# An attention kernel that also makes the residual sum, its statistics and its router products

## The reference, cut to what matters

```python
x = x + 0.5 * ffn(layernorm(x))         # x: (8, 2048, 256)
x = x + attention(layernorm(x))         # 8 heads of 32, rank 32 projections
x = x + 0.5 * ffn(layernorm(x))

def ffn(x):                             # x is already normalized
    scores = x @ w_router
    _, idx = top_k(scores, 128)         # 128 of 2048 tokens of each batch
    x_sel = take(x, idx)
    ...                                 # small attention and gated FFN on x_sel
    return x.at[idx].set(x_sel + x_attn + x_ff)
```

## Time and profile before

| what | us |
|---|---|
| median of 3 runs | 4373.87 |
| the profiled execution, its own time | 4375.15 |
| its span, first to last instruction | 4373.6 |
| s2 with its entry (3847.0 to 4018.6) | 171.6 |
| t2 (4018.6 to 4096.0) | 77.4 |
| f2 (4096.0 to the end) | 278 |
| a steady unit of `attend` | 46.7 |

### The profile page before, as it was taken

One profiled execution on the slowest core, in us unless ns is written; L12 is line 12 of the kernel. 1 busy time (PEld: TensorE's weight loads), 2 busy tenths in 40 slices (PEclk: granted clock), 3 DMA queues, 4 the chain that ended last, 5 costly groups with the idle time before them and its releaser, 6 DMA issues. The chain is left out here.

```text
span 4373.6 us, 59760 instructions
## 1 busy us (share of the span) xinstructions
PE 3589.1 (82%) x20178; PEld 1423.8 (33%) x20178; DVE 3267.7 (75%) x4504; ACT 3208.9 (73%) x6587; POOL 2938.5 (67%) x1094
## 2 busy tenths in 40 slices
PE   0167685599999999999999999999999999900376
PEld 0133463233333333333333333333333333300243
DVE  9644575788888888888888888888888888368544
ACT  5044474498898998998998898998988988723143
POOL 0011000399999999999999999999999999952211
PEclk9998898699999999999999999999999999955588
DMA  8200699689999999999999999999999998877100
GB/s 280 89 3 5 212 395 341 130 180 192 208 199 205 206 199 205 198 209 203 200 208 195 207 198 205 206 199 207 197 208 204 201 205 186 169 249 249 39 5 5
DMA packets 335171, 809.45 MB, mean 185 GB/s; under 512 B 27084, under 2 KB 210912, under 8 KB 271136
## 3 DMA queue, kind: packets, MB, share of 16 engines
q0 software_dynamic: 66432, 475.04, 53.9%
q1 hardware_dynamic: 222496, 284.46, 22.2%
q10 hardware_dynamic: 45952, 46.27, 3.0%
HBM read 198.90 MB, written 136.48 MB: 77 GB/s over the span
## 5 line engine op out<-in xcount | busy, mean ns | idle before, releaser
L1682 ACT ACTIVATE at_probs<-at_ps_s 128x512 f32<-128x512 f32 x4096 | 2262.1, 615 | 254.7 <-PE at_ps_s L1792 247.3
L1541 POOL TENSOR_TENSOR at_pool_sum<-at_pool_sum,at_probs 128x2048 f32<-128x2048 f32 x448 | 2173.0, 4850 | 30.9 <-DMA at_probs<-at_probs 23.5
L1571 DVE TENSOR_REDUCE at_part_max<-at_ps_max 128x3 f32<-128x1536 f32 x1024 | 1801.3, 1759 | 426.8 <-PE at_ps_max L1715 426.7
L1792 PE MATMUL at_ps_s<-at_qs,at_ks 97*128 97x512 f32 (+1 forms) x4096 | 1523.4, 451 | 6.2 <-ACT at_probs L1682 4.9
L1761 PE MATMUL at_ps_acc<-at_probs,at_v 128*32 128x512 f32 x8192 | 1091.8, 605 | 0.9 <-ACT at_probs L1682 0.9
L1792 PEld LDWEIGHTS at_ps_s<-at_qs,at_ks 97*128 97x128 f32 (+1 forms) x4096 | 626.1, 188 | 1102.4 <-ACT at_probs L1682 815.9
L1573 DVE TENSOR_REDUCE at_part_max<-at_max_copy 128x1 f32<-128x512 f32 x1024 | 692.1, 676 | 0.0
L1634 ACT COPY at_max_copy<-at_ps_max 128x512 f32<-128x512 f32 x1024 | 610.1, 596 | 102.2 <-PE at_ps_max L1715 102.1
L1715 PE MATMUL at_ps_max<-at_ks,at_qs 32*128 32x512 f32 x4096 | 525.4, 500 | 83.0 <-DMA at_ks<-qk_parts 49.3
L1520 POOL DMA_DIRECT2D at_probs<-at_probs x448 | 399.3, 891 | 284.5 <-ACT at_probs L1682 236.7
L1715 PEld LDWEIGHTS at_ps_max<-at_ks,at_qs 32*128 32x128 f32 x4096 | 197.8, 183 | 442.1 <-issue 386.0
(11 more groups left out here) (193 smaller groups left out, 2550.0 us busy)
## 6 DMA issues: line engine op xcount, KB each, us to landing
at_probs<-at_probs POOLq DMA_DIRECT2D x448, 1024.0 KB, 8.3
qk_parts<-pr_hi SPq DMA_DIRECT2D x32, 1024.0 KB, 12.0
qk_parts<-pr_lo SPq DMA_DIRECT2D x32, 1024.0 KB, 12.5
at_qs<-qk_parts SPq DMA_DIRECT2D x320, 64.0 KB, 5.8
at_ks<-qk_parts SPq DMA_DIRECT2D x80, 256.0 KB
s_x<-in_x SPq DMA_DIRECT2D x16, 1024.0 KB
after_ffn<-s_y ACTq DMA_DIRECT2D x16, 1024.0 KB, 6.8
v_tokens<-pr_v SPq DMA_DIRECT2D x32, 512.0 KB, 11.0
```

Of the source, the lines that this page charges most:

```text
L1541: nc.gpsimd.tensor_tensor(acc, first, probs[:, slot(unit, c)], ALU.add).then_inc(pool_added, 1)
L1571: nc.vector.reduce_max(part_max[:, 0:HG - 1, t, c], ps_max[:, 0:HG - 1], AX.X).then_inc(three_max_done, 1)
L1682: nc.scalar.activation(probs[:, slot(unit, c), h], ps_s[:, BANK[unit, j]], ACT.Exp, scale=SCALE).then_inc(exp_done, 1)
L1792: nc.tensor.matmul(ps_s[:, BANK[unit, j]], ks[rows, g, h, c * P:(c + 1) * P], qs[rows, unit % NQB, h, :], start=True, stop=True).then_inc( ...
```

## The change

`attend` now takes `after_ffn` too. For each unit SP loads the matching 512 half rows into `x` (`load_x`), POOL adds them to `o` (`add_x`, a tensor_tensor of 128x512), SP stores the sum to `hidden`, and in the unit after that DVE takes `bn_stats` and the router product of its four tiles of 128x128. The router's weights lie in SBUF here. Three tiles are done in cycle 6 ahead of `invert`, the statistics of the fourth in cycle 9 and its product in cycle 11. To make room the ring of chunk buffers has 8 instead of 9, and a chunk takes the buffer that a table (`READ_BY`) says is free first. Stage s2 becomes `scores_of_stats`, which reads no rows: it combines the statistics that `attend` left in SBUF. The output rows are made by ACT inside t2 (`finish`), loaded from `hidden` and stored by ACT's own queue while DVE picks the tokens. f2 gathers from `hidden` alone.

```diff
+READ_BY = (8, 8, 11, 8, 13, 9, 15, 11, 17, 13, 19, 15, 21, 17, 23, 19)
...
+def chunk_buffers(units, ring):
+    read_by, owner, buffer, before = [(-1, k) for k in range(ring)], {}, {}, {}
+    for unit in range(units):
+        for c in range(NCYC):
+            read_by.sort()
+            _, k = read_by.pop(0)
+            buffer[unit, c], before[unit, c], owner[k] = k, owner.get(k), (unit, c)
+            read_by.append((unit * NCYC + READ_BY[c], k))
+    return buffer, before
...
-    RING = 9
+    RING = 8
...
-                sp.wait_ge(o_done, unit + 1)
+                sp.wait_ge(h_done, unit + 1)
...
+            def add_x(unit):
+                k = unit % 2
+                pool.wait_ge(x_in, unit * 16 + 16)
+                pool.wait_ge(o_done, unit + 1)
+                h = o[:, k].rearrange("p t h d -> p t (h d)")
+                nc.gpsimd.tensor_tensor(h, h, xt[:], ALU.add).then_inc(h_done, 1)
...
                     start_pair(unit, d)
+                    if unit > 0 and d == 2:
+                        add_x(unit - 1)
...
+                nc.vector.bn_stats(stats[:, b, g, u * QT + t, :], half_row(unit, t)).then_inc(stats_done, 1)
...
+                nc.vector.tensor_tensor_reduce(out=scratch[:].bitcast(F32), in0=w[:, g * P:(g + 1) * P],
+                                               in1=half_row(unit, t), scale=1.0, scalar=0.0, op0=ALU.mult, op1=ALU.add,
+                                               accum_out=products[:, b, g, u * QT + t:u * QT + t + 1]
+                                               ).then_inc(products_done, 1)
...
+                        if unit > 1 and i == CLOSE_IN:
+                            score_tiles(unit - 2, range(QT - 1))
+                        if unit > 1 and i == CLOSE_IN + 3:
+                            stats_of(unit - 2, QT - 1)
+                        if unit > 1 and i == CLOSE_IN + 5:
+                            products_of(unit - 2, QT - 1)
...
+        if finish is not None:
+            @block.scalar
...
+                for b in range(AHEAD):
+                    load(b)
+                for b in range(B):
...
+                        for t in range(half * HALF, (half + 1) * HALF):
+                            last = nc.scalar.activation(rows[:, k, t, :], rows[:, k, t, :], ACT.Identity,
+                                                        scale=affine[:, b, 0, t:t + 1], bias=affine[:, b, 1, t:t + 1])
+                        last.then_inc(y_done, 1)
+                        act.wait_ge(y_done, 2 * b + half + 1)
+                        act.dma_start(y[tokens, :].rearrange("(t p) d -> p t d", p=P), rows[:, k, tiles]
+                                      ).then_inc(y_out[k], 16)
...
-        attend(nc, "at", qk, v_dram, attention)
...
+                attend(nc, "at", qk, v_dram, after_ffn, w_router, stats, products, hidden)
+                scores_of_stats(nc, "s2", stats, products, w_router, scores)
...
-            score_pass(nc, "s2", after_ffn, attention, w_router, out, scores)
-            pick_tokens(nc, "t2", scores, picked[:], weights)
-            routed_ffn(nc, "f2", after_ffn, attention, picked[:], weights, out)
+            pick_tokens(nc, "t2", scores, picked[:], weights, (hidden, products, out))
+            routed_ffn(nc, "f2", hidden, None, picked[:], weights, out)
```

More of the change, by code:

```diff
@@ L347, in load, with pick_tokens @@
         queue.dma_start(vb[:], v_bias.partition_broadcast(P)).then_inc(self.loaded, 16)
-def pick_tokens(nc, tag, scores, picked, weights):
+def pick_tokens(nc, tag, scores, picked, weights, finish=None):
     QUARTERS = 4
@@ L406, in pick_tokens @@
         picked_done = sem("picked_done")
+        if finish is not None:
+            h, affine, y = finish
+            NBUF, AHEAD = 4, 2
+            HALF = T // 2
+            rows = sb("rows", [P, NBUF, T, D])
+            h_in = [sem(f"h_in{i}") for i in range(2 * NBUF)]
+            y_done = sem("y_done")
+            y_out = [sem(f"y_out{i}") for i in range(NBUF)]
         block = ctx.enter_context(nc.Block())
@@ L481, in _, with part, load @@
             dve.wait_ge(picked_done, 1)
+        if finish is not None:
+            @block.scalar
+            def _(act):
+                def part(b, half):
+                    first = b * S + half * HALF * P
+                    return slice(first, first + HALF * P), slice(half * HALF, (half + 1) * HALF)
+                def load(b):
+                    k = b % NBUF
+                    if b >= NBUF:
+                        act.wait_ge(y_out[k], b // NBUF * 32)
+                    for half in range(2):
+                        tokens, tiles = part(b, half)
+                        act.dma_start(rows[:, k, tiles], h[tokens, :].rearrange("(t p) d -> p t d", p=P)
+                                      ).then_inc(h_in[2 * k + half], 16)
+                for b in range(AHEAD):
+                    load(b)
+                for b in range(B):
+                    k = b % NBUF
+                    if b + AHEAD < B:
+                        load(b + AHEAD)
+                    for half in range(2):
+                        tokens, tiles = part(b, half)
+                        act.wait_ge(h_in[2 * k + half], b // NBUF * 16 + 16)
+                        for t in range(half * HALF, (half + 1) * HALF):
[5 more added lines that the diff above has]
+                                      ).then_inc(y_out[k], 16)
+                for k in range(NBUF):
+                    act.wait_ge(y_out[k], 32 * len(range(k, B, NBUF)))
         @block.tensor
@@ L1290, in score_banks, with attend @@
     return bank, after
-def attend(nc, tag, qk, v_dram, out):
+READ_BY = (8, 8, 11, 8, 13, 9, 15, 11, 17, 13, 19, 15, 21, 17, 23, 19)
[8 more added lines that the diff above has]
+    return buffer, before
+def attend(nc, tag, qk, v_dram, x, w_router, stats, products, out):
     UQ = 512
@@ L1320, in attend @@
     BANK, AFTER = score_banks(B * BU, TILES, PER_CYC)
+    BUFFER, BEFORE = chunk_buffers(B * BU, RING)
     def slot(unit, c):
-        return (unit * NC + c) % RING
+        return BUFFER[unit, c]
     def adds_through(c):
@@ L1351, in attend @@
         neg_max = sb("neg_max", [P, HG * QT])
-        max_row = sb("max_row", [HG * QT, P], F32R)
-        ones = sb("ones", [P, P])
+        scratch = sb("scratch", [P, P], F32R)
+        max_row = scratch[0:HG * QT]
+        ones = sb("ones", [P, DH])
         ident = sb("ident", [P, P])
@@ L1482, in batch @@
                         store(unit - 1, b - 1, BU - 1)
+                    if unit > 0:
+                        load_x(b, un)
                     if u < NU - 1 and ahead:
@@ L1654, in free @@
                     def free(c):
-                        before, k = divmod(unit * NC + c - RING, NC)
+                        if BEFORE[unit, c] is None:
+                            return
+                        before, k = BEFORE[unit, c]
                         act.wait_ge(pv_done, before * NC + k + 1)
@@ L1678, in batch @@
                         c, h = divmod(j, HG)
-                        if h == 0 and (carry or c >= RING):
+                        if h == 0:
                             free(c)
```

142 lines of the change are left out of this document (135 added, 7 removed).

## The result

| | median us (runs) | ratio to before [95%] |
|---|---|---|
| before | 4373.06 (4364.55 to 4378.55, 4) | |
| after | 4535.48 (4521.38 to 4564.07, 4) | 1.0379 [1.0343, 1.0416] |

A forecast was written before the change was run, and what follows sets the result against it. PE was taken to bound attend, busy 199.75 of 200 us. From 4375.15 us, 131.9 gained outside attend's units and 227 lost to held products and buffers gave 4470, 4469 for the median; range 4370 to 4580.

The forecast's parts named there:

- The sign and the mechanism: In attend, products with both inputs in SBUF wait for POOL's addition and stop PE; slower by over 0.2%, chance 0.80.
- The deciding term: In attend, held products stop PE 2.6 us in cycle 6, 1.1 in cycle 11; 3.5 taken for 62 units, 217 us.
- whatever stops PE is paid in full: In attend, PE is busy 199.75 of 200 us at 2.4 GHz, so each stop costs its length, 64 times.
- The buffers: In attend, the ring of 8 makes chunk 4 wait 1.7 us in 16 units: 27 us, shrinking to 10.
- Behind `attend`: Stages after attend: s2 gains 155.6 us, t2 costs 32.6 more, f2 gains 11.4.
- (d): End of attend: sum with x before the last store, four tiles of statistics and products after it; 2.5 us added.
- What would show it: Signs: product median well over 1 us, maximum near 4.9; statistics near 0.3; PE awaiting the reciprocal; units about 50 us.
- 1: Rival in attend: the product is not held; 4279 us, faster by 2.2%; chance 0.16.
- 2: Rival in attend: cycle 6's three products each wait for an addition, some 9.8 us more per unit; 5077 us; chance 0.04.
- 3: Rival in attend: products held but meeting less of each addition, 1.9 us a unit; 4370 us; chance 0.05.

The follow-up runs named there:

- e1: The changed kernel with all four statistics in cycle 6 and all four products behind normalize in cycle 7, in POOL's idle time: 4332.19 us, ratio 0.9884.
- e2: The changed kernel with each router product replaced, in its place, by a one-input reduce_sum of the row tile; scores not the reference's: 4325.7 us, ratio 0.9898.
- e6: The changed kernel with statistics and products of all four tiles ahead of the inverse in cycle 6: 4569.77 us, ratio 1.0435.
- e11: The changed kernel with only the fourth tile moved: statistics into cycle 6, product behind normalize in cycle 7: 4545.82 us, ratio 1.0395.
- e5: e2 plus one DVE reduction of 3.88 us, one input in SBUF, ahead of the first statistics in cycle 6: 4526.14 us, ratio 1.0352.
- e3: The kernel before with only the ring changed, 8 chunk buffers by the table instead of 9 in turn: 4404.4 us, ratio 1.0068.
- e12: The changed kernel with the last number of the buffer table 20 instead of 19, products left in place: 4551.11 us, ratio 1.0385.
- e10: e9 with t2's row loads issued by SP instead of ACT, four batches ahead instead of two: 4288.29 us, ratio 0.9792.
- e9: e1 with the last number of the buffer table 20 instead of 19: 4294.91 us, ratio 0.9818.
- e4: The changed kernel with the residual sum alone: no statistics or products in attend, s2 the full score pass on hidden: 4394.17 us, ratio 1.0044.

## Why the prediction was right, point by point

**The sign and the mechanism** were right: an instruction with two inputs in SBUF is held while POOL adds, PE stops for the reciprocal, and the loss is larger than the 132 us gained behind `attend`. e1 and e2 show it from two sides, by taking away the collision and by taking away the second input. The Trainium skill (SBUF — State Buffer, Who interferes with whom) says that one of the two waits for all of the other; the trace agrees, with 4.13 us for the product that came 0.9 us into an addition of 4.87.

**The deciding term** was mis-sized. "Together 3.7 us a unit. I take 3.5" stands, in the profiled execution, against 3.15 of stops (cycle 6 at 49.2 - 46.8 = 2.4 by e6 and e11, where 2.6 was forecast, and cycle 11 at 0.7 instead of 1.1), and against 2.0 more a unit that it didn't contain: 62 x 3.15 = 195 and 62 x 2.0 = 125, together the 320 measured, where 229.5 were expected. By the prediction's own range of 2.4 to 5 us a unit the stops lie inside and the 5.17 of both together just outside. The step that failed is "whatever stops PE is paid in full": it is paid more than in full. PE was busy 199.75 of 200 us before, and its clock was taken as a given of the stage. That is where the median's 66 us over the forecast come from, since the stops alone were forecast a little too long. e5 makes a loss of the same size, 4526, with a plain instruction of 3.88 us in that place.

**The buffers.** The 27 us alone were right (e3: 29.5), the place too, chunk 4. Whether they "shrink to 10" beside held products or to nothing, e12 can't tell: it shows no gain, and 10 us lie within its spread.

**Behind `attend`.** s2 was forecast at 16 us and is 12.5. t2 was forecast at 110, is 116.6 here, and is 106.3 in e10: the rate was right, the time in which ACT issues loads was missing. f2 gained 14.0 instead of 11.4. Together they gave 159.1 - 39.2 + 14.0 = 133.9 us, where 134.4 were forecast for the three; (d) lies within `attend` and wasn't measured apart.

**What would show it.** "A median well over 1 us" was wrong in form, since two products of four meet no addition and the fourth does at 1.6; the mean is 1.61 us and the maximum 5.4. The wait for the reciprocal, the statistics at 0.28, the unit of 50 us at full clock and ACT's wait at chunk 4 came as written.

**The rivals.** 1 (not held, 4279) is out by the product's 4.13 us. But its price is that of a kernel with the buffers' loss in which nothing is held: e2 is that kernel with 4326, 47 us above, and e9, without that loss, has 4295. 2 is out by e6. 3 (1.9 us a unit) is out: the first product of a unit is held for 4.13 us in the median and 4.06 in the mean, so it meets nearly the same part of the addition in nearly every unit.

**Still open:** what the late keys and POOL's late sum cost in e9, each by itself, and why some units of the same kernel lose the clock and others, with the same stop, don't.

## What to carry to other kernels

Before an instruction is put into another engine's idle time, ask what it reads: with two operands in SBUF it belongs where POOL is idle, and its duration alone does not price it. The same instructions cost 3.8% in cycles 6 and 11 and saved 1.2% in cycle 7. Look at every unit and not only at the median one: a single product that came 0.2 us behind a pair, and not ahead of it, cost its unit 8.6 us. Where an engine is busy all the time, ask what a stop brings with it beside its own length, here the clock of PE. And try a shared resource's change in a kernel where it can be seen: a table's number worth 37 us in one version showed nothing in the other.

## What the runs showed of the hardware beyond that

- A granted clock of 1.00 over 2600 us fell to 0.96 (after, e5) and 0.94 (e6), when PE, busy almost without a break before, stood idle for 2.6 to 3.1 us in each unit of some 50 (0.1 before), 1.7 to 2.1 of them in one stop. In the unit at 2102.7 of after the stop of 1.71 us ends at 2126.21, one of 0.49 at 2127.82, and a piece of 13.7 us at half clock begins at 2128.29, 2.1 us behind the first. Over 60 units of after this adds 2 us to each, beside the stop itself. In its Part 1 the page TensorE: Matmul & The Clock Gate of the Trainium skill says that "the default state is throttled, and activity releases the throttle". e5 is in line with it: beside e2 it has one instruction of DVE more, PE's busy time in 2600 us falls from 2552 to 2465, and the clock goes from 0.99 to 0.96.
- No run shows that the collision also lengthens POOL's addition. The first product starts 0.9 us into one, and that addition takes 4.87 us, as it does elsewhere. Additions of 5.2 to 5.3 us, like the one below, occur beside products of cycle 11, but also in before (up to 5.30) and in e4, which has no product in `attend`. So the longer product of cycle 11, 2.1 instead of 1.6, goes with an addition that ends later; what lengthens that one stays open.

```profile
2034.92 5.21 POOL L1724 TENSOR_TENSOR at_pool_sum<-at_pool_sum,at_probs 128x2048 f32<-128x2048 f32 x1
...
2038.18 2.10 DVE L1804 CUSTOM_DVE_ANT_0 at_scratch<-at_w,at_o 128x128 f32<-128x128 f32 x1
```

- In t2 ACT needs 19.1 us to issue its first four loads, of 1 MB each, and computes nothing meanwhile; with SP issuing them its first rows begin 14 us earlier.
